# Graph network on one core: a finished block of the pair-count matrix leaves in three transfers instead of one

## The reference

```python
# stage L0: both directions of every edge through a three-layer MLP, summed at the nodes, then three GRU cells
agg  = segment_sum(mlp(cat[x[src], x[dst], edge]), dst) + segment_sum(mlp(cat[x[dst], x[src], edge]), src)
s1 = gru0(x, agg); s2 = gru1(agg, s1); s3 = gru2(s1, s2)
x = layernorm(x + s3)
# stage L1: three layers of neighbour sums over the same edges
for l in range(3):
    S = segment_sum(X[src], dst)
    X = relu(((1 + eps[l]) * X + S) @ W1[l] + b1[l]) @ W2[l] + b2[l]
x = layernorm(x + X)
```

## Time and profile before

| | |
|---|---|
| median of 3 runs | 2401.57 us |
| profiled execution, device time | 2405.81 us |
| its span | 2403.9 us |
| turns of the edge stage | 104 |
| transfers `adj<-band` in the turns | 25, of 1500 KB (the first 750 KB) |
| granted TensorE clock, mean | 0.982 |

### The profile page before, as it was taken

The page is one execution under the profiler, slowest core; times in us unless marked ns, Lnnn a source line. Parts: engine busy times, 40 slices in busy tenths (PEclk is TensorE's granted clock), DMA queues, the critical chain, the costliest instruction groups (busy, mean ns, idle before and its releaser), DMA issues. The chain is left out here.

```text
span 2403.9 us, 39417 instructions
## 1 busy us (share of the span) xinstructions
PE 2278.5 (95%) x12547; PEld 1876.2 (78%) x12547; DVE 1761.2 (73%) x4056; ACT 1230.7 (51%) x2106; POOL 1143.2 (48%) x846
## 2 busy tenths in 40 slices
PE   4999999999999999999999999999999879799997
PEld 3888888888888888888888888888888645588886
DVE  7888888888888888888888888888887557602114
ACT  4556556656656656556666566565665413211112
POOL 2556555656566666566566565665665300000000
PEclk9999999999999999999999999999999979899998
DMA  4356556446555445555535555544555450395873
GB/s 161 80 106 131 98 94 109 87 80 110 98 94 111 90 78 109 95 97 108 96 77 106 94 110 97 94 95 87 103 103 94 59 218 1 118 385 229 337 286 142
DMA packets 232338, 292.57 MB, mean 122 GB/s; under 512 B 126016, under 2 KB 189862, under 8 KB 223800
## 3 DMA queue, kind: packets, MB, share of 16 engines
q1 hardware_dynamic: 158756, 237.04, 36.0%
q0 software_dynamic: 73216, 54.58, 16.9%
q10 hardware_dynamic: 272, 0.05, 0.0%
HBM read 218.51 MB, written 73.08 MB: 121 GB/s over the span
## 5 line engine op out<-in xcount | busy, mean ns | idle before, releaser
L470 POOL DMA_INDIRECT sums<-outb,target x416 | 671.1, 1613 | 625.0 <-ACT outb L640 421.6
L463 POOL DMA_INDIRECT xg<-in_x,gidx x416 | 467.4, 1123 | 158.8 <-issue 140.9
L1237 PEld LDWEIGHTS ebank<-w3t,h 128*128 128x128 f32 x3328 | 387.4, 192 | 8.3 <-issue 0.3
L1237 PE MATMUL ebank<-w3t,h 128*128 128x128 f32 x3328 | 388.2, 275 | 0.2 <-ACT h L622 0.2
L1225 PE MATMUL ebank<-h1h,w2h 128*128 128x512 f32 x832 | 365.0, 439 | 5.1 <-DVE h1l L849 3.3
L622 ACT ACTIVATE h<-ebank,b2c 128x512 f32<-128x512 f32 x416 | 286.6, 689 | 116.2 <-issue 81.9
L608 ACT ACTIVATE h1h<-hpre 128x512 fp32r<-128x512 f32 x416 | 257.9, 628 | 154.6 <-DVE hpre L845 115.7
L1225 PE MATMUL ebank<-h1h,w2l 128*128 128x512 f32 x832 | 328.9, 395 | 0.0
L1225 PE MATMUL ebank<-h1l,w2h 128*128 128x512 f32 x832 | 326.3, 392 | 0.0
L849 DVE SCALAR_TENSOR_TENSOR h1l<-hpre,h1h 128x512 fp32r<-128x512 f32 x416 | 270.9, 691 | 17.2 <-ACT h1h L608 13.6
L845 DVE TENSOR_TENSOR hpre<-pb,ebank 128x512 f32<-128x512 f32 x416 | 265.1, 677 | 2.3 <-PE ebank L1211 2.2
(11 more groups left out here) (266 smaller groups left out, 3800.6 us busy)
## 6 DMA issues: line engine op xcount, KB each, us to landing
ring<-adj SPq DMA_DIRECT2D x54, 1568.0 KB, 8.4
rowb<-along SPq DMA_DIRECT2D x104, 512.0 KB
adj<-band SPq DMA_DIRECT2D x25, 1500.0 KB
ef<-in_edge_attr SPq DMA_DIRECT2D x103, 256.0 KB
stay<-adj SPq DMA_DIRECT2D x6, 1568.0 KB, 14.4
xg<-in_x,gidx POOLq DMA_INDIRECT x416
sums<-outb,target POOLq DMA_INDIRECT x416
sums<-band SPq DMA_DIRECT2D x2, 1664.0 KB
```

Source lines behind the costliest of these rows:

```text
L463: pool.indirect_dma_start(out=to, out_offset=None, in_=a["x"], in_offset=bass.IndirectOffsetOnAxis(ap=ids, axis=0)).then_inc(s_x[par], 16)
L470: pool.indirect_dma_start(out=tables[k % 2], out_offset=bass.IndirectOffsetOnAxis(ap=target[par][:, 1, k:k + 1], axis=0), in_=outb[par][:, ...
L1237: last = nc.tensor.matmul(bank[6 + way][:, t * P:(t + 1) * P], h2[:, way, k, t * P:(t + 1) * P], w3t[:, k, :], start=not bias and k == 0, ...
```

## The change

Each block is stored by three transfers instead of one. `THIRDS` divides the 25 panels into 9, 8 and 8; every transfer carries all 120 columns of its panels, still in pieces of 480 bytes. They are issued after `reload` of three tiles in a row (the first at the place of the old transfer), and each still waits for the same count of `s_acc`. Only for the last block that is stored within the turns are all three issued at one place. ACT's three clears stay where they are and each clears the panels of one transfer (9 x 120 = 1080 or 8 x 120 = 960 elements instead of 1000), after a wait for that transfer alone. The two blocks stored after the last turn stay as they are.

```diff
+THIRDS = ((0, 9), (9, 17), (17, NB))
...
-                def flush(i, b, lo):
+                def flush(i, b, third, lo=0):
 
                     sp.wait_ge(s_acc, i * 8)
                     c = (i - 2) * BLK + BLK // 2
-                    sp.dma_start(panels_of(adj_flat)[:, :, bass.ds(c + lo, BLK - lo)],
-                                 band_of(slots(b) + lo, slots(b) + BLK)).then_inc(s_flush, 16)
-
-                def turn(g, par, half, event=None):
+                    some = slice(*THIRDS[third])
+                    sp.dma_start(panels_of(adj_flat)[:, some, bass.ds(c + lo, BLK - lo)],
+                                 band_of(slots(b) + lo, slots(b) + BLK)[:, some, :]).then_inc(s_flush, 16)
+
+                def turn(g, par, half, *events):
                     reload(g, par, half)
-                    if event:
+                    for event in events:
                         flush(*event)
...
-                    turn(g, g % 2, g // 2, (1, -1, BLK // 2) if g == 6 else None)
+                    turn(g, g % 2, g // 2, *([(1, -1, g - 6, BLK // 2)] if 6 <= g < 9 else []))
                 later.load(sp, a)
                 with sp.Fori(0, ROUNDS) as m:
                     for q in range(12):
                         turn(m * 12 + (10 + q), q % 2, m * 6 + (5 + q // 2),
-                             (m * 3 + (2 + q // 4), q // 4, 0) if q % 4 == 0 else None)
+                             *([(m * 3 + (2 + q // 4), q // 4, q % 4)] if q % 4 < 3 else []))
                 for g in range(10 + 12 * ROUNDS, G - 1):
-                    turn(g, g % 2, g // 2, ((g - 2) // 4, (g - 2) // 4 - 2, 0) if g % 4 == 2 else None)
+                    i, third = divmod(g - 2, 4)
+                    turn(g, g % 2, g // 2, *[(i, i - 2, t) for t in range(3) if t == third or (g == G - 2 and t > third)])
...
-                sp.wait_ge(s_flush, (ITERS + 1) * 16)
+                sp.wait_ge(s_flush, (3 * (ITERS - 1) + 2) * 16)
...
                 def clear(i, b, third):
 
-                    act.wait_ge(s_flush, i * 16)
-                    lo = slots(b) + third * (BLK // 3)
-                    nc.scalar.copy(band_of(lo, lo + BLK // 3), none[:, 0:BLK // 3].unsqueeze(1)
-                                   .broadcast_to([P, NB, BLK // 3])).then_inc(s_fresh, 1)
+                    act.wait_ge(s_flush, i * 48 + (third * 16 - 32))
+                    some = slice(*THIRDS[third])
+                    nc.scalar.copy(band_of(slots(b), slots(b) + BLK)[:, some, :], none[:, 0:BLK].unsqueeze(1)
+                                   .broadcast_to([P, some.stop - some.start, BLK])).then_inc(s_fresh, 1)
```

## The result

The changed kernel takes 2394.89 us (median of 20 runs, 2390.53 to 2397.73), the kernel before 2401.62 us beside it (20 runs, 2397.04 to 2407.49). The ratio is 0.9969 (95% interval 0.9962 to 0.9977): 6.7 us less, clear of the 0.2% that can be told from no change. The forecast was 2395.0.

A forecast was written before the change was run, and what follows sets the result against it. PE was taken to bound the edge stage, with turns behind a store lengthened by late adds. 2405.8 - 6.6 = 2399.2 us for the profiled execution; the median, 4.2 lower, gives 2395.0 us, range 2388 to 2403.

The forecast's parts named there:

- What bounds the turns, and that L924 is the way from a store to PE: Edge stage: PE busy 1625.70 of 1648.30 us; late adds reach PE through DVE's L924, 12 waits, 10.6 us.
- So adds issued by 401.5 land when the burst ends: One store's turn: POOL's adds issued beside the burst land only at its end, so L924 waits until 413.65.
- the ring was full: SP behind a store: the next index load takes 7.02 us to issue instead of some 0.35.
- The twelfth, 1.8 us in the turn from 1829.2, stays: L924's wait where three transfers go out together: burst as long as before, following turn keeps its 19.1 us.
- Shorter bursts: DMA in store turns: engines through some 10 us into the turn; 11 of L924's 12 waits go, 8.8 us.
- 6.6 us from the turns: PE's gain: 23 turns without a clear fall from 18.06 us each to 17.775.
- SP, the clears, the 1080 elements: 50 more SP transfers at 0.63 us of issue each and ACT's resized clears: cost 0.
- Rival A: Gain lost in the spread, L924's waits stay because engines alternate between queues by packet: 2397 to 2404 us, chance 0.32.
- Rival B: Adds delayed by any burst starting beside them, L924 waits in three turns of four: +21, 2423 us, chance 0.06.

The follow-up runs named there:

- late store: Kernel before, its store still one transfer but issued later, behind the fourth add: 2409.42 us, ratio 0.9956 to the kernel before.
- three at once: Changed kernel with all three transfers of a block issued one behind the other at the old place: ratio to the kernel before 0.9902, rerun 0.9911.
- wrap late again: Rerun of the changed kernel with DVE's `wrap` moved from ahead of `onehot` to behind `ways(g + 1)`: 2366.89 us, ratio 0.9864 to the kernel before.
- clears alone: Kernel before with only the clears changed, to the panels of `THIRDS`: 2419.56 us, ratio 0.9999 to the kernel before.

## Why the prediction was right, and where not

- **What bounds the turns, and that L924 is the way from a store to PE:** right. No store, or no wait of L924, and the turns without a clear are as short as the others; in late store they are too, but there other turns are longer, and the loss was only moved.
- **"So adds issued by 401.5 land when the burst ends":** this is the step that failed. In the earlier trace rows burst and transfer were one and the same, so the rows could not tell which of them delayed the adds; three at once has the same bytes in one burst and 3 waits in place of some 19. What counted was that they went out as one transfer, or with a long one first. For the changed kernel both readings give the same answer, for 24 of 25 stores. That the ring was full was a reading too: the rows have the 7.02 us, and no view shows the ring.
- **"The twelfth, 1.8 us in the turn from 1829.2, stays":** wrong for the same reason. Three transfers stand there at one place, L927 doesn't wait, and the next turn took 17.60 us. It isn't always so: in wrap late again L927 waits 1.0 us at this place, and the next turn takes 18.2.
- **Shorter bursts:** the DMA share behind a third falls under 0.6 some 8 us into the turn (0.41 from 399.8 on, in a turn that begins at 391.8); I had said 10. No wait of L924 is left.
- **6.6 us from the turns:** the 23 turns of the sum lost 6.7 in the profile; the last turn, which was to keep its 19.1 us, lost 1.6 more; and the median of the comparison moved by 6.7. But the term was taken from one profile with 12 waits, and that the comparison was made in the same kind of session is luck. The kernel before had 19 waits in session 3, where the gain is 24 us, and clears alone 20 in session 1, where three at once was 25 us faster than the kernel before. The term was worked out well and is no property of the change; a profile of the kernel before from another session would have shown its spread. What makes it 12 or some 20 was not found.
- **SP, the clears, the 1080 elements:** cost nothing that shows, as said; clears alone is at 0.9999.
- **Rival A** rested on the packet rule of the Trainium skill ("DMA: Bandwidth & Descriptors", Queues, rings and completion order), by which POOL's adds would not mind SP's burst. The trace disagrees with what was drawn from it: not a packet of q0 in 6 us beside a busy q1, with gathers issued. Whether q0 had packets ready for the engines in that time no view shows, so the rule itself is not tested. That part of A, with waits of L924 that stay, is refuted. Its other part, that the turns of 18.0 us are about as large as the gain, was the truth about the noise: 33 and 35 of 64 in the first pair, none in the pair of session 3.
- **Rival B** would have needed waits in the turns of the second and third transfer; there are none, even with each third sent twice (the place with six transfers at once aside).

The version to keep is the changed kernel with the late `wrap`: 2366.89 us, against 2374.54 for the changed kernel and 2398.41 for the kernel before in the same session.

## What to carry to other kernels

A large transfer of small pieces on one queue can hold up another engine's queue for several microseconds. Here cutting it into three like parts cost nothing that could be measured and took the harm away, even with the parts one behind the other; cutting off only a small rest did not, and moving the transfer to a later place only moved the stall. Look for the cost of such a burst in the turn behind it, in a wait of an engine that isn't the bottleneck, and measure the length of the turns and not the idle time of the busy engine. Before a term of a few microseconds is trusted, look at an execution from another session: here the count of the stalls was 12 in one and 19 in the other, for one kernel.

## What the runs showed of the hardware

- Beside a transfer of 3200 pieces of 480 bytes on SP's queue (q1), POOL's queue (q0) moved no packet from 4 to 10 us behind its issue at the store shown, while q1 moved 730 in 3 us; the mean over 24 stores is some 4 a microsecond or fewer from 4 to 9 us.
- The turns come in two lengths, 17.54 and 18.0 us. The 0.45 us are ACT's second copy of `es` (L633) starting late: in the changed kernel of session 0, PE's L1240 ends 11.03 us into the turn in both kinds, and the copy starts at 11.07 in the short ones and 11.48 in the long ones (means). In sessions 0 and 1 about half of the turns are long, with or without stores; in sessions 2 to 4 next to none, also for the same program, which is 20 us of 2400 (the changed kernel, 2394.89 and 2374.54). What decides was not found; sessions 1 and 2 name the same chip.
- A stall can cost more than itself. In the kernel before of session 3, L924 waits 2.78 us, until 412.1. PE stands idle for 1.8 us until 415.2, and from 416.4 its granted clock is 0.50 (1.2 of 2.4 GHz) for 3.4 us; the turn from 411.4 takes 21.3 us, where those behind waits of 2.5 to 2.7 us elsewhere take 19.7 to 20.1 at a full clock. Windows of that turn, columns as in the earlier trace rows:

```profile
411.40:414.40 3.00, 1.97 (x11) 1.00 0.58 122
416.40:419.70 3.30, 3.30 (x9) 0.50 0.23 20
419.80:423.80 4.00, 4.00 (x26) 1.00 0.36 49
```

- 1.1 us of DVE work ahead of `onehot`, 8 times, cost 1.0 us of PE each; at the end of DVE's turn it cost nothing. In `wrap late again` the eight turns take 17.54 us.
